# Two row halves of a head on even and odd partitions, in the loads of q and k

## What is computed

```python
q = (query @ Wq).reshape(b, t, h, d)          # h = 32 heads, d = 128
k = (key @ Wk).reshape(b, t, kv_h, d)         # kv_h = 8
v = (value @ Wv).reshape(b, t, kv_h, d)
q = apply_rope(q)
k = apply_rope(k)
q = q.reshape(b, t, kv_h, g, d)               # g = 4 query heads share a key head
logits = jnp.einsum('btkgd,bTkd->bkgtT', q, k)
logits = 30.0 * jnp.tanh(logits * ATTN_MULT / 30.0)
weights = softmax(where(mask, logits, -1e+30))
attn = jnp.einsum('bkgtT,bTkd->btkgd', weights, v)
```

## Time and profile before

| | |
|---|---|
| median of 3 runs | 2150.35 us (2149.82 to 2153.23) |
| profiled execution | 2158.16 us |
| its span, first to last instruction | 2156.4 us |
| mean granted clock of TensorE in it | 0.997 |
| PE busy in it | 2132.3 us, 99% |
| DVE, ACT, GpSimd busy | 78%, 41%, 14% |
| bytes moved by DMA | 508.50 MB, mean 236 GB/s |

### The profile page before, as it was taken

One profiled execution on the slowest core, in us unless ns is written; L12 is line 12 of the kernel. 1 busy time (PEld: TensorE's weight loads), 2 busy tenths in 40 slices (PEclk: granted clock), 3 DMA queues, 4 the chain that ended last, 5 costly groups with the idle time before them and its releaser, 6 DMA issues.

```text
span 2156.4 us, 26390 instructions
## 1 busy us (share of the span) xinstructions
PE 2132.3 (99%) x9429; PEld 1729.3 (80%) x9429; DVE 1674.3 (78%) x2571; ACT 883.1 (41%) x1342; POOL 294.0 (14%) x359
## 2 busy tenths in 40 slices
PE   9999999999999999998999999999999999999999
PEld 7888888888888888876777877777787777888887
DVE  6976888888886666676877779997999879857443
ACT  3323243222241111155565556655666556423221
POOL 0350001111131000012101111111112111100000
PEclk9999999999999999999999999999999999999999
DMA  8698697665596665698666885689767965696741
GB/s 327 234 332 290 218 334 271 231 221 211 209 339 229 211 212 201 221 279 263 189 193 196 233 224 174 202 273 276 194 195 221 298 182 163 210 368 265 294 184 66
DMA packets 207987, 508.50 MB, mean 236 GB/s; under 512 B 20720, under 2 KB 54128, under 8 KB 205808
## 3 DMA queue, kind: packets, MB, share of 16 engines
q1 hardware_dynamic: 187376, 443.31, 62.7%
q0 software_dynamic: 20480, 63.50, 9.3%
HBM read 357.26 MB, written 149.16 MB: 235 GB/s over the span
## 4 chain that ended last, share of the span: by engine, by line
PE 87%; DMA 7%; DVE 3%; ACT 1%; issue 1%; SPq 0%; POOL 0%; DVEq 0%; ACTq 0%
PE ps L377 28%; PE ps L378 28%; PE ps L379 28%; DMA RB<-rD 3%; DMA rD<-r 2%; PE ps L920 1%; DMA X2D<-stg 1%; DMA raw<-gran 1%; DVE Y L990 1%; DMA Y<-xT 1%; DVE Rl L330 1%; DVE ps L330 0%; DVE ps L905 0%; DVE Pl L330 0%; DMA kraw<-ctxT 0%
## 5 line engine op out<-in xcount | busy, mean ns | idle before, releaser
L377 PE MATMUL ps<-Ah,Rh 128*128 128x512 f32 x1024 | 400.9, 391 | 4.2 <-DVE Y L990 4.2
L378 PE MATMUL ps<-Al,Rh 128*128 128x512 f32 x1024 | 399.9, 391 | 0.0
L379 PE MATMUL ps<-Ah,Rl 128*128 128x512 f32 x1024 | 399.5, 390 | 0.0
L379 PE MATMUL ps<-Xq,qW 128*128 128x512 f32 x896 | 348.6, 389 | 0.0
L377 PE MATMUL ps<-Xq,qW 128*128 128x512 f32 x896 | 348.5, 389 | 0.0
L378 PE MATMUL ps<-Xq,qW 128*128 128x512 f32 x896 | 348.5, 389 | 0.0
L330 DVE TENSOR_TENSOR Rl<-raw,Rh 128x1024 fp32r<-128x1024 f32 x174 | 212.2, 1220 | 57.6 <-ACT Rh L326 57.2
L326 ACT ACTIVATE Rh<-raw 128x1024 fp32r<-128x1024 f32 x176 | 185.5, 1055 | 154.6 <-PE ps L379 127.1
L377 PEld LDWEIGHTS ps<-Ah,Rh 128*128 128x128 f32 x1024 | 193.2, 189 | 46.8 <-DVE Y L990 4.6
L379 PEld LDWEIGHTS ps<-Ah,Rl 128*128 128x128 f32 x1024 | 193.1, 189 | 40.8
L378 PEld LDWEIGHTS ps<-Al,Rh 128*128 128x128 f32 x1024 | 193.2, 189 | 40.5
(11 more groups left out here) (217 smaller groups left out, 3881.7 us busy)
## 6 DMA issues: line engine op xcount, KB each, us to landing
raw<-gran SPq DMA_DIRECT2D x177, 512.0 KB, 5.6
QSD<-qW SPq DMA_DIRECT2D x64, 512.0 KB, 3.1
qD<-qt SPq DMA_DIRECT2D x128, 256.0 KB, 3.3
qW<-QSD SPq DMA_DIRECT2D x64, 512.0 KB, 3.7
qf<-qD SPq DMA_DIRECT2D x64, 512.0 KB, 8.5
RB<-rD POOLq DMA_DIRECT2D x128, 256.0 KB, 6.8
qraw<-gran SPq DMA_DIRECT2D x48, 512.0 KB, 4.3
kD<-kst SPq DMA_DIRECT2D x32, 512.0 KB, 3.8
```

Source lines behind the costliest of these rows:

```text
L377: put("pe", waits, lambda e: e.matmul(pe_out, lh, rh, start=first, stop=False, skip_group_check=more))
L378: put("pe", [], lambda e: e.matmul(pe_out, lh, rl, start=False, stop=False, skip_group_check=more))
L379: return put("pe", [], lambda e: e.matmul(pe_out, ll, rh, start=False, stop=last, skip_group_check=more), mark)
```

## The change

The two halves `s` of q and of k no longer go to partitions 0 to 63 and 64 to 127. Row `p` of half `s` goes to partition 2p + s. `P` is 128. Both tiles have the same order of dimensions, before and after. Nothing else is touched: number, size and source of the transfers, the queue, the waits, and the instructions of all engines and their order are the same.

```diff
         def att_load_qk(gi):
             c, g = groups[gi]
             n = gi % 2
-            f_marks[gi] = [dma(qf[n][64 * s:64 * s + 64, :, :], qD[c, g, s].rearrange("h p t -> p h t"),
+            f_marks[gi] = [dma(qf[n][s:P:2, :, :], qD[c, g, s].rearrange("h p t -> p h t"),
                                att_in["f"][n] + q_store[c, g], f"d_qf{n}{s}", 512) for s in range(2)]
-            k_marks[gi] = [dma(f(kT[n][64 * s:64 * s + 64, :, :]), kD[c, s, :, g].rearrange("l p t -> p l t"),
+            k_marks[gi] = [dma(f(kT[n][s:P:2, :, :]), kD[c, s, :, g].rearrange("l p t -> p l t"),
                                att_in["k"][n] + k_store[c], f"d_kt{n}{s}", 256) for s in range(2)]
```

## The result

The changed kernel takes 2132.05 us (median of 4 runs, 2129.11 to 2133.58), the kernel before beside it 2151.63 (4 runs, 2149.82 to 2153.23). The ratio is 0.9908, 95% interval 0.989 to 0.9925: 19.6 us or 0.9% faster. The profiled execution took 2132.16 us.

The account below looks back on a forecast made before the run. PE's waits in the attention and the lowered clock were taken as the bound. Terms 7.2 + 3.4 + 0.8 + 3.4 = 14.8 us, cut to 9.8, gave 2150.35 - 9.8 = 2140.5, rounded to 2141; range 2136 to 2152.

Parts of the forecast that it names:

- What bounds the kernel: In the attention, PE's waits (16.1 us) and the lowered clock behind four of them (7.0 us) limit the gain.
- What a load costs: Loads into 64 partitions run at half rate; full rate could save up to 1.27 us per `qf` half, 0.54 per `kT` half.
- The saving taken as two thirds: For q and k loads in the attention, 0.85 us saved per `qf` half and 0.36 per `kT` half.
- the four terms: Savings at the attention's start, 7.2 us, and at the sample changes at 1270, 1504 and 1734 us: 3.4, 0.8, 3.4.
- The wait for `qt`: Before 940 us, PE's wait of 0.8 us for DVE's `qt` was to stay.
- The floor: For the profiled execution, at most 23.1 us could be saved, so it couldn't go below 2135.1 us.
- The step from the profiled execution to the median: Whole kernel: 7.8 us were taken as stalls other runs lack, so the gain of 14.8 us became 9.8.
- The clock: At 1270 and 1734 us, a remaining wait of 1.0 us would keep the full clock, saving 1.75 us more each.
- the third rival: At 1504 us, `RB` over 1.6 us later lengthens PE's wait past 2.4 us, bringing the slow clock; 2157 us, chance 0.08.
- the halves still meet: In the changed loads, engines still meet in pairs and the rate stays near 206 GB/s; 2150 us, chance 0.14.
- Hidden anyway: In the attention, GpSimd's own pace holds the `RB<-rD` chain, so PE's waits stay; 3 us gain, 2147 us, chance 0.12.
- Slower: In the attention, `raw` and `Y` loads move up and delay `RB<-rD`; up to 6.6 us lost, 2157 us, chance 0.08.

Follow-up runs that it names:

- the two runs with reach and step taken apart: Kernel before, halves changed: one across partitions 32 to 95, the other in two transfers, 2142.51 us; or every second partition, each transfer within one side of 64, 2153.78 us.
- k alone: Kernel before with only the k loads sent to every second partition, q still in two halves: 2143.41 us, ratio 0.9953.
- q alone: Kernel before with only the q loads sent to every second partition, k still in two halves: 2135.28 us, ratio 0.9904.
- the 21 other groups: Kernel before with the change only for groups not loaded at the attention's start or shortly before a change of the sample: 2149.33 us, ratio 0.9966.
- 11 of 32 groups: Kernel before with the change only for groups loaded at the attention's start or in the 60 us before a sample change's waits: 2133.15 us, ratio 0.9891.

## Why the prediction was wrong

The direction and the mechanism were right; the sizes were wrong. The forecast lacks 9.8 us. Of these, 8.4 are missing in the sum for the profiled execution (23.2 us where I had 14.8): 3.5 because I took two thirds of the saving per load, 4.1 because I put the cost of a split set of sum matmuls at nothing, and 0.8 for a wait that was to stay. The other 1.4 lie in the step from there to the median (a deduction of 3.6 where I took 5.0).

*What bounds the kernel*: right. The gain came from PE's waits in the attention, the clock behind them and the sum matmuls that the waits split; q stage and feed-forward stage are as before.

*What a load costs*: right, and it is what the gain rests on. Half the rate goes with half the partitions, shown by the two runs with reach and step taken apart.

*The saving taken as two thirds*: wrong, it is all of it. I took 0.85 us per `qf` half and 0.36 per `kT` half, because only half the rows of a neighbourhood are written at a time. Measured are 407 and 406 GB/s, so 1.27 and 0.54, the upper bounds. Three of the four terms grow, by 3.5 us together: at 1270 and 1734 us the waits go wholly (2.7 and 3.0 where I took 1.7 each), and at the start 6.6 us of waits and one slow stretch go, 8.35 where I took 7.2. The full saving doesn't explain all of this: two `qf` halves give 2.5 us, less than the 3.0 at 1734 us. The terms counted only that pair; by the one profile with k alone, loads further ahead count too.

*The wait for `qt`*: wrong, but small. The 0.8 us before 940 us were to stay. No profile of the changed kernel has this wait; with q alone it is 0.3 us, with k alone 0.7. Why it went was not followed up.

*The floor*: wrong. 2158.16 - 23.1 = 2135.1 was to be the least, and the changed kernel's own profile has 2132.16. The price of a wait was taken as its idle time and the clock behind it. Waits in the midst of the sum matmuls cost 4.1 us beyond that, since a split set keeps PE busy longer. I had put this at nothing; the price stood in the trace as busy time, not as a wait. And the first 20 us were slower by 2.5 us in that one execution, with no connection to the change: the same kernel's other profile has 63 matmuls there, not 49. The lower end of the range, 2136, rested on the same 23.1 us.

*The step from the profiled execution to the median*: wrong in size. I took the 7.8 us between them to be stalls that the other runs don't have, and cut the sum from 14.8 to 9.8. Waits do differ between executions, as the repeated profile shows. But 2.5 of the 7.8 us were the start, and three runs were too few to say what is ordinary: three later sets on three chips, 42 runs of the kernel before, have medians of 2152.78 to 2156.15. Whether the number of runs or the chip makes this difference was not tried. The profile's own pieces that the change brought are 13.9 + 5.25 + 4.07 = 23.2 us; the measured 19.6 need a deduction of 3.6 from them.

*The clock*: not tested where it entered the sum. A wait of 1.0 us was to keep the full clock at 1270 and 1734 us, but no wait is left there; in the repeated profile of the kernel before, the waits of 1.1 us (line 920) and 1.4 us (`Y`) kept it. The 2.4 us that the third rival used as a limit doesn't hold: the wait of 2.2 us in the changed kernel was followed by 1.2 GHz.

*The rivals*: "the halves still meet" fell, at the first short stretch (407 GB/s). With it fell the estimate beside it of 0.15 us saved per half: measured are 1.27 us, with transfers of q that reach only 64 of the 128 partitions each, and the measurement decides. "Hidden anyway" fell: PE's waits went with the loads. "Slower" fell: `RB<-rD` lands in 6.0 us in the median. "In the rest of the attention faster loads are worth nothing" held for most of it; the 21 other groups gave some 6 us, which I had put at zero.

## What to carry to other kernels

A transfer into one half of the partitions ran here at half the rate (184 to 232 GB/s against 405 to 407) although all DMA engines were busy; if a tile must come in two transfers, let each reach both sides of partition 64, and permute the rows of both matmul operands alike. Look for the places where PE waits while the DMA share is near 1: there bytes per second count (11 of 32 groups brought the whole gain), elsewhere they hardly do. When a wait falls into a set of matmuls that run side by side, its price is more than its idle time (here 1.04 us more). And a profiled execution whose time stands apart from the runs should be repeated before a forecast is cut to fit.

## What the runs showed of the hardware that I had not expected

Interleaved rows cost nothing: 64 rows on every second partition reach 407 GB/s, as 128 rows do (410). Sixty-four neighbouring rows across the middle (32 to 95) take the same 84 ns to a packet of 2 KB; the rate read there, 358 GB/s, is that of a stretch of 0.6 us.

Transfers of 32 rows inside one half move 228 to 232 GB/s, no less than 64 rows in that half: what counts is the half, not the number of rows.

The spread of the times shrank as the waits went. On one chip, 11 runs of the kernel before reach from 2143.55 to 2161.78 us, six of the changed kernel from 2129.84 to 2136.03.
